# Mixture-of-experts blocks written to their tokens' places from inside the loop, with the second matrix read in place by TensorE

## The reference

```python
logits = t @ switch_w + switch_b
route_prob = softmax(logits); route_prob_max = max(route_prob); routes = argmax(route_prob)
for e in range(8):
    h = gelu(t @ w1[e] + b1[e])            # 128 -> 512
    y = h @ w2[e] + b2[e]                  # 512 -> 128
    out = where(routes == e, y, out)
out = out * route_prob_max                 # and then x = x + out
```

## Time and profile before

| what | value |
|---|---|
| time, median of 3 runs (lowest to highest) | 1508.23 us (1506.53 to 1508.61) |
| the profiled execution: its own time | 1510.94 us |
| the profiled execution: span from first to last instruction | 1509.1 us |
| TensorE busy | 1114.1 us (74%) |
| VectorE busy | 970.7 us (64%) |
| ScalarE busy | 696.1 us (46%) |
| GpSimd busy | 519.0 us (34%) |
| granted TensorE clock, mean | 0.871 of full speed |
| layer 0: scatter, loop, gather and norm | from 212.8, 254.5, 350.4 to 410.3 us |
| layer 1: scatter, loop, gather and output | from 1322.9, 1364.6, 1461.9 to 1509.1 us |

### The profile page before, as it was taken

The page is one execution under the profiler, slowest core; times in us unless marked ns, Lnnn a source line. Parts: engine busy times, 40 slices in busy tenths (PEclk is TensorE's granted clock), DMA queues, the critical chain, the costliest instruction groups (busy, mean ns, idle before and its releaser), DMA issues. The chain is left out here.

```text
span 1509.1 us, 31316 instructions
## 1 busy us (share of the span) xinstructions
PE 1114.1 (74%) x9281; PEld 992.8 (66%) x9281; DVE 970.7 (64%) x2930; ACT 696.1 (46%) x1448; POOL 519.0 (34%) x396
## 2 busy tenths in 40 slices
PE   3595321992264799999999999999999997607960
PEld 2494221881133698988889888898888985506850
DVE  6886930553472677787777777777787776503532
ACT  2144510551171466666666666666666663103430
POOL 1500125005200544444444444444444441071016
PEclk9998555996585999999999999999999998557985
DMA  8000031221068464746546465564655610211113
GB/s 220 0 0 1 1 143 47 61 57 49 26 232 220 114 154 119 163 121 140 145 125 161 113 150 134 129 162 111 158 131 129 158 33 2 112 61 53 56 52 99
DMA packets 85256, 156.21 MB, mean 104 GB/s; under 512 B 9056, under 2 KB 65824, under 8 KB 76512
## 3 DMA queue, kind: packets, MB, share of 16 engines
q1 hardware_dynamic: 81120, 147.33, 37.6%
q0 software_dynamic: 4096, 8.40, 1.9%
HBM read 127.51 MB, written 28.18 MB: 103 GB/s over the span
## 5 line engine op out<-in xcount | busy, mean ns | idle before, releaser
L1109 POOL TENSOR_SCALAR ds_scores<-ds_scores,ds_max 128x256 f32<-128x256 f32 x256 | 348.5, 1361 | 396.1 <-DVE ds_max L1301 396.0
L1293 DVE TENSOR_TENSOR ds_p2c<-ds_bank,ds_p2c 128x512 f32<-128x512 f32 x256 | 175.8, 687 | 95.5 <-PE ds_bank L1146 95.5
L1242 ACT ACTIVATE all_xt<-ds_bank 128x512 f32<-128x512 f32 x256 | 152.9, 597 | 152.0 <-PE ds_bank L1164 152.0
L1137 PE MATMUL ds_bank<-ds_qr,ds_tab 128*128 128x128 f32 x1536 | 189.1, 277 | 21.6 <-DVE ds_qr L1277 19.9
L1137 PE MATMUL ds_bank<-ds_kr,ds_tab 128*128 128x128 f32 x1536 | 198.6, 276 | 0.6 <-ACT ds_p2c L1226 0.6
L1137 PEld LDWEIGHTS ds_bank<-ds_qr,ds_tab 128*128 128x128 f32 x1536 | 180.9, 194 | 23.5 <-issue 23.4
L1301 DVE CUSTOM_DVE_ANT_0 ds_scores<-ds_bank,ds_p2c 128x256 f32<-128x256 f32 x512 | 195.3, 417 | 0.2 <-DVE ds_p2c L1293 0.2
L1226 ACT ACTIVATE ds_c2p_t<-ds_bank 128x512 f32<-128x512 f32 x256 | 152.7, 596 | 91.7 <-PE ds_bank L1137 90.5
L1137 PEld LDWEIGHTS ds_bank<-ds_kr,ds_tab 128*128 128x128 f32 x1536 | 185.0, 193 | 1.0 <-issue 0.8
L1226 ACT ACTIVATE ds_p2c<-ds_bank 128x512 f32<-128x512 f32 x256 | 149.2, 597 | 54.2 <-PE ds_bank L1137 54.1
L1146 PE MATMUL ds_bank<-all_constants,ds_c2p_t 128*128 128x128 f32 x1024 | 157.6, 276 | 0.0
(11 more groups left out here) (236 smaller groups left out, 1711.5 us busy)
## 6 DMA issues: line engine op xcount, KB each, us to landing
ds_qr<-scratch_qk SPq DMA_DIRECT2D x32, 1024.0 KB, 10.9
ds_kr<-scratch_qk SPq DMA_DIRECT2D x32, 1024.0 KB, 13.7
ds_tab<-scratch_tables SPq DMA_DIRECT2D x64, 248.0 KB, 9.8
ds_qs<-scratch_q_parts SPq DMA_DIRECT2D x32, 288.0 KB
ds_ks<-scratch_k_parts SPq DMA_DIRECT2D x32, 288.0 KB
slots_in<-all_zero SPq DMA_DIRECT2D x2, 2560.0 KB, 15.4
0f_weights<-expert_rows SPq DMA_DIRECT2D x1, 4112.0 KB, 13.2
1f_weights<-expert_rows SPq DMA_DIRECT2D x1, 4112.0 KB, 13.3
```

Source lines behind the costliest of these rows:

```text
L1109: pool.tensor_scalar(S[b % NS][:, 1, :], S[b % NS][:, 1, :], mx[:, 2 * b + 1:2 * b + 2], None, ALU.subtract).then_inc(s_sub1, 1)
L1137: last = pe.matmul(pb[n % 2][:, a * P:(a + 1) * P], TAB[half][:, kind, c:c + P], mov[:, :].rearrange("p (b g s) -> p g b s", b=HALF, s=16) ...
L1242: act.activation(PT[b], pt2[:, :].rearrange("p (k s) -> p k s", k=2), ACT.Exp).then_inc(s_exp, 1)
L1293: dve.tensor_tensor(z, pt1[b % 2][:, :].rearrange("p (a k) -> p a k", a=2), z, ALU.add).then_inc(s_z, 1)
```

## The change

The change does these things:

- A row in the slots gets 258 numbers in place of 128: the normalised token, the token itself (`X_AT`), the count of tokens left (`LEFT_AT`: 4096 minus the token's own number, so that the zeros of a padding slot mean "none"), and its probability (`PROB_AT`). `XN`, `X` and the two columns become one tile, `rows`. The zero fill grows to the same width.
- In the loop VectorE's `result` has three operations in place of one: y plus bias as before, the token's number from `LEFT_AT`, and y times probability plus the token itself. The last waits for the first.
- GpSimd scatters each block's `y` by these numbers to its tokens' places in the loop (`store`), 40 indirect transfers with a bounds check that leaves out padding. The target is the output in layer 1 and a DRAM tensor `tokens` in layer 0. SP's stores to `slots_out` go, and so do the 32 gathers, the tile `G` and the 32 additions behind the loop.
- In layer 0 SP loads `X` back from `tokens` in four transfers, one for each group of the norm.
- SP's load of `xb` for block k waits until y(k-4) is written, where it waited for the transpose of k-4, as the additions read `xb` too.
- `WB` holds the first matrix and the biases (644 columns). TensorE reads the second matrix in `WA` at a register of its own, which it loads from `bexp` in each `down`.
- The experts' matrices arrive in three transfers in place of two, and the zero fill is issued behind the linear attention's weights.

Core of the diff (the two loads of a layer's matrices, the constant `left` and renamed arguments left out):

```diff
-W1_AT, W2_AT, B1_AT, B2_AT = 0, F, F + FC * D, F + FC * D + FC
-EXPERT_COLS = B2_AT + D
+W1_AT, B1_AT, B2_AT, W2_AT = 0, F, F + FC, F + FC + D
+COPY_COLS, EXPERT_COLS = W2_AT, W2_AT + FC * D
+
+
+X_AT, LEFT_AT, PROB_AT = D, 2 * D, 2 * D + 1
+ROW = 2 * D + 2
...
         def _(pool):
+            def store(g, i):
+                pool.wait_ge(s_y, UNROLL * g + i + 1)
+                pool.indirect_dma_start(tokens, bass.IndirectOffsetOnAxis(ap=token[i][:, 0:1], axis=0), y[i][:, :], None,
+                                        bounds_check=TOKENS - 1, oob_is_err=False).then_inc(s_out[i], 16)
             pool.wait_ge(s_cleared, 16)
             for t in range(TILES):
                 pool.indirect_dma_start(slots_in, bass.IndirectOffsetOnAxis(ap=slot[:, t:t + 1], axis=0),
-                                        norm.XN[:, t, :], None).then_inc(s_scat, 16)
-            for i in range(UNROLL):
-                pool.wait_ge(s_out[i], 16 * GROUPS)
-            for t in range(TILES):
-                pool.indirect_dma_start(G[:, t, :], None, slots_out,
-                                        bass.IndirectOffsetOnAxis(ap=slot[:, t:t + 1], axis=0)).then_inc(s_gath[t // GQ], 16)
+                                        rows[:, t, :], None).then_inc(s_scat, 16)
+            for k in range(BLOCKS):
+                store(k // UNROLL, k % UNROLL)
 
         @block.sync
         def _(sp):
             sp.wait_ge(s_scat, 16 * TILES)
 
-            def rows(g, i):
-                wait_over(sp, s_xt, UNROLL * (g - 1) + i + 1)
+            def load(g, i):
+                wait_over(sp, s_y, UNROLL * (g - 1) + i + 1)
                 sp.dma_start(xb[i][:, :], slots_in[bass.ds((UNROLL * g + i) * P, P), :]).then_inc(s_x[i], 16)
-            def store(g, i):
-                sp.wait_ge(s_y, UNROLL * g + i + 1)
-                sp.dma_start(slots_out[bass.ds((UNROLL * g + i) * P, P), :], y[i][:, :]).then_inc(s_out[i], 16)
-
-
-            def step(g, i):
-                rows(g, i)
-                if not isinstance(g, int) or g > 0:
-                    store(g - 1, i)
-
-            over_blocks(sp, step)
+            over_blocks(sp, load)
             for i in range(UNROLL):
-                store(GROUPS - 1, i)
-            if finish is not None:
+                sp.wait_ge(s_out[i], 16 * GROUPS)
+            if again:
+                back = tokens.rearrange("(t p) d -> p t d", p=P)
                 for q in range(TILES // GQ):
-                    sp.wait_ge(s_fin, GQ * (q + 1))
-                    sp.dma_start(finish[:, q * GQ:(q + 1) * GQ, :], X[:, q * GQ:(q + 1) * GQ, :]).then_inc(s_stored, 16)
-                sp.wait_ge(s_stored, 16 * (TILES // GQ))
+                    sp.dma_start(rows[:, q * GQ:(q + 1) * GQ, X_AT:X_AT + D], back[:, q * GQ:(q + 1) * GQ, :]).then_inc(s_back[q], 16)
...
             def down(g, i):
                 k = UNROLL * g + i
                 wait_over(pe, s_y, k - 1)
+                e = pe.value_load(bexp[0:1, bass.ds(k, 1)], min_val=0, max_val=E - 1)
                 for c in range(FC):
                     pe.wait_ge(s_g, FC * k + c + 1)
-                    last = pe.matmul(py[i % 2][:, 0:D], h[i % 2][:, c, :], WB[i][:, W2_AT + c * D:W2_AT + (c + 1) * D], start=(c == 0), stop=(c == FC - 1))
+                    last = pe.matmul(py[i % 2][:, 0:D], h[i % 2][:, c, :], WA[:, bass.ds(e, 1), W2_AT + c * D:W2_AT + (c + 1) * D].rearrange("p a n -> p (a n)"), start=(c == 0), stop=(c == FC - 1))
                 last.then_inc(s_yp, 1)
...
@@ -414,18 +409,23 @@
             def expert(g, i):
                 e = dve.value_load(bexp[0:1, bass.ds(UNROLL * g + i, 1)], min_val=0, max_val=E - 1)
                 wait_over(dve, s_y, UNROLL * (g - 1) + i + 1)
-                dve.tensor_copy(WB[i][:, :], WA[:, bass.ds(e, 1), :].rearrange("p a n -> p (a n)")).then_inc(s_wb, 1)
-
-            def rows(g, i):
+                dve.tensor_copy(WB[i][:, :], WA[:, bass.ds(e, 1), 0:COPY_COLS].rearrange("p a n -> p (a n)")).then_inc(s_wb, 1)
+
...
             def result(g, i):
-                dve.wait_ge(s_yp, UNROLL * g + i + 1)
+                k = UNROLL * g + i
+                dve.wait_ge(s_yp, k + 1)
                 wait_over(dve, s_out[i], 16 * g)
-                dve.tensor_tensor(y[i][:, :], py[i % 2][:, 0:D], WB[i][:, B2_AT:], ALU.add).then_inc(s_y, 1)
+                dve.tensor_tensor(y[i][:, :], py[i % 2][:, 0:D], WB[i][:, B2_AT:COPY_COLS], ALU.add).then_inc(s_yb, 1)
+                dve.tensor_scalar(token[i][:, :], xb[i][:, LEFT_AT:LEFT_AT + 1], -1.0, float(TOKENS), ALU.mult, ALU.add)
+                dve.wait_ge(s_yb, k + 1)
+                dve.scalar_tensor_tensor(y[i][:, :], y[i][:, :], xb[i][:, PROB_AT:PROB_AT + 1], xb[i][:, X_AT:X_AT + D],
+                                         ALU.mult, ALU.add).then_inc(s_y, 1)
...
-            for t in range(TILES):
-                if t % GQ == 0:
-                    dve.wait_ge(s_gath[t // GQ], 16 * GQ)
-                dve.scalar_tensor_tensor(X[:, t, :], G[:, t, :], prob[:, t:t + 1], X[:, t, :], ALU.mult, ALU.add).then_inc(s_fin, 1)
-                if finish is None and t % GQ == GQ - 1:
-                    dve.wait_ge(s_fin, t + 1)
-                    norm.vector(dve, t // GQ)
-            if finish is None:
+            if again:
+                for q in range(TILES // GQ):
+                    dve.wait_ge(s_back[q], 16)
+                    norm.vector(dve, q)
                 norm.vector(dve, norm.GROUPS)
...
@@ -527,6 +523,7 @@
             for j in range(2):
                 sp.dma_start(gain[:, j, :], w[f"g{j + 1}"].partition_broadcast(P)).then_inc(s_gb, 16)
                 sp.dma_start(bias[:, j, :], w[f"b{j + 1}"].partition_broadcast(P)).then_inc(s_gb, 16)
+            clear_slots(sp)
...
     x = dram["L0_attn_a_x"].rearrange("b (u p) d -> p (b u) d", p=P)
-    y = out.rearrange("b (u p) d -> p (b u) d", p=P)
+    y = out.rearrange("b s d -> (b s) d")
-        X = m.sb("x", [P, TILES, D])
+        rows = m.sb("rows", [P, TILES, ROW])
+        XN, X = rows[:, :, 0:D], rows[:, :, X_AT:X_AT + D]
...
-                sp.wait_ge(s_zero, 1)
-                for slots, s_cleared in zip(slots_in, s_clear):
-                    sp.dma_start(slots.rearrange("(p b) d -> p b d", p=P), zero[:, :].unsqueeze(1).to_broadcast([P, BLOCKS, D])).then_inc(s_cleared, 16)
...
+        def clear_slots(sp):
+            sp.wait_ge(s_zero, 1)
+            for slots, s_cleared in zip(slots_in, s_clear):
+                sp.dma_start(slots.rearrange("(p b) d -> p b d", p=P), zero[:, :].unsqueeze(1).to_broadcast([P, BLOCKS, ROW])).then_inc(s_cleared, 16)
```

More of the change, by code:

```diff
@@ L269, in _, with run_experts @@
             then(dve.tensor_scalar(bexp[:, :], bexpf[:, :], float(E - 1), None, ALU.min))
-def run_experts(nc, prefix, X, norm, con, WA, s_weights, prob, slot, bexp, slots_in, slots_out, s_cleared, finish):
+def run_experts(nc, prefix, rows, norm, con, WA, s_weights, slot, bexp, slots_in, tokens, s_cleared, again):
     with ExitStack() as stack:
@@ L278, in run_experts @@
         UNROLL = 4
-        WB = [m.sb(f"expert_{i}", [P, EXPERT_COLS]) for i in range(UNROLL)]
-        xb = [m.sb(f"xb_{i}", [P, D]) for i in range(UNROLL)]
+        WB = [m.sb(f"expert_{i}", [P, COPY_COLS]) for i in range(UNROLL)]
+        xb = [m.sb(f"xb_{i}", [P, ROW]) for i in range(UNROLL)]
         xbt = [m.sb(f"xbt_{i}", [P, P]) for i in range(2)]
@@ L283, in run_experts @@
         y = [m.sb(f"y_{i}", [P, D]) for i in range(UNROLL)]
-        G = m.sb("gathered", [P, TILES, D])
+        token = [m.sb(f"token_{i}", [P, 1], U32) for i in range(UNROLL)]
         bank = m.banks(8)
         px, ph, py = bank[0:2], bank[2:4], bank[4:6]
-        if finish is None:
+        if again:
             norm.begin(bank[6:8])
-        s_fin, s_stored = m.sem("finished"), m.sem("stored")
-        s_wb, s_xt, s_xtc, s_h, s_g, s_yp, s_y = (m.sem(n) for n in ("wb", "xt", "xtc", "h", "gelu", "yp", "y"))
+        s_wb, s_xt, s_xtc, s_h, s_g, s_yp, s_yb, s_y = (m.sem(n) for n in ("wb", "xt", "xtc", "h", "gelu", "yp", "yb", "y"))
         s_scat = m.sem("scattered", own=True)
         GQ = norm.GT
-        s_gath = [m.sem(f"gathered{q}", own=True) for q in range(TILES // GQ)]
+        s_back = [m.sem(f"back{q}", own=True) for q in range(TILES // GQ)]
         s_x = [m.sem(f"x{i}") for i in range(UNROLL)]
-        s_out = [m.sem(f"out{i}") for i in range(UNROLL)]
+        s_out = [m.sem(f"out{i}", own=True) for i in range(UNROLL)]
         GROUPS = BLOCKS // UNROLL
@@ L1429, in shape_constants @@
         "iota_b": np.broadcast_to(np.arange(BLOCKS), (P, BLOCKS)),
+        "left": TOKENS - row[:, None] - P * np.arange(TILES)[None, :],
     }
@@ L1463, in program @@
         logits = m.sb("logits", [P, TILES, E])
-        zero = m.sb("zero", [P, D])
+        zero = m.sb("zero", [P, ROW])
         s_zero = m.sem("zero")
-        slots_in = [nc.dram_tensor(f"slots_in{layer}", (SLOTS, D), FP32, kind="Internal").ap() for layer in range(2)]
```

(3 more changed lines are left out.)

47 lines of the change are left out of this document (23 added, 24 removed).

## The result

The changed kernel takes 1460.05 us (median of 4 runs, 1458.41 to 1461.5) against 1508.42 for the one before: ratio 0.967, 95% interval 0.965 to 0.970. It is 48 us faster; I had forecast 64.

A forecast was written before the change was run, and what follows sets the result against it. It took a circle of TensorE and VectorE to bound the loop. Start -1, layer 0's tail -35.4, layer 1's -42.3 and loop +14.4 sum to -64.3 us, giving 1444 us; range 1424 to 1484.

The forecast's parts named there:

- the bound of the kernel before: Expert loop: a circle of TensorE and VectorE, 9.10 us for four blocks; whatever is added counts once for two blocks.
- the tails: Behind each layer's last result: without the gathers, 35.4 us saved in layer 0 and 42.3 in layer 1.
- VectorE's terms: Loop, each hop of two blocks: +0.35 us for the longer result, -0.30 for the narrower copy.
- the rivals with GpSimd: Loop: GpSimd's store holds VectorE's copy (1486 us, chance 0.15), or GpSimd itself becomes the bound (1460 us, chance 0.1).
- GpSimd becomes the bound: Loop: stores wait for VectorE to leave the memory port, 2.66 us a block, +16, 1460 us; chance 0.1.
- the step on the cover of the rows' load: Loop: rows lie there 5.0 us after up(k-3), the transpose needs them at 5.7; cover 0.7, so no cost.
- both of my terms: Loop: the later rows covered by 0.7 us, at no cost, and TensorE's register load at +0.31 us a hop.
- the transposes wait for rows: Loop: a sign that the prediction is wrong, if TensorE's transposes wait for the later-loaded rows.
- the register load of TensorE: Loop, ahead of down: the load alone, +0.31 us a hop; bounds 0 and 0.88.
- the start: Linear attention's start: zero fill moved behind its weights saves 1 us; 0 to 2 possible.

The follow-up runs named there:

- w2_copied: Changed kernel with VectorE copying all 1156 columns again and TensorE reading the second matrix from the copy without a register load: 1445.3 us, ratio 0.957.
- direct_store: Changed kernel with SyncE storing results block after block in slot order in place of GpSimd's indirect stores, the results' own places left out: 1449.4 us, ratio 0.959.
- in_place_only: Kernel before with only the second matrix read in place through TensorE's register load and VectorE copying 644 columns; gathers and stores as before: 1512.4 us, ratio 1.002.
- split_rows: Changed kernel with each block's rows loaded in two transfers, the transpose's 128 columns early, the rest when the result is written: 1443.0 us, ratio 0.956.
- before_fill_moved: Kernel before with only the zero fill, at its old width, issued behind the linear attention's weights: 1506.6 us, ratio 0.9992.

## Why the prediction was right, and where it was wrong

**Right: the bound of the kernel before, and the tails.** Without the gathers the tails got 34.9 us shorter (forecast 35.4) and 40.8 (42.3). Of the 1.5 missing in layer 1, 0.97 is the last store's later start and 0.6 the drain.

**Right: VectorE's terms.** Multiply-add 0.33 behind the addition (0.35 forecast), the narrower copy 0.27 less on the way to xbt (0.30), nothing held by the stores. w2_copied shows them in the period: 2.44 against 2.26 + 0.175.

**Right: the rivals with GpSimd are out.** The copy starts 0.86 behind the multiply-add's start (1.2 to 1.3 at the loop's turn, as in the kernel before) and takes 0.50; the stores take 1.04. That the time, 1460, is the one that I had worked out for "GpSimd becomes the bound" is chance: direct_store keeps layer 1's period without GpSimd. Part of it was also easier on the stores than I had thought: a store starts 0.79 behind the multiply-add's end and not 0.2, so it meets only the last 0.2 us of the copy. It takes 1.04 there, 0.98 with no copy beside it, and 1.29 in w2_copied, where the copy of 1156 columns runs beside it for some 0.5 us. That is 0.3 us more and lies in GpSimd's idle time. It is not the 2.5 more (3.1 in place of 0.62) that the Trainium skill ("SBUF — State Buffer", "SBUF: two separate sides") has beside a copy, whose length it does not give.

**Wrong: the step on the cover of the rows' load.** I wrote that the rows lie there 5.0 after up(k-3) and are needed 5.7 after it, a cover of 0.7. The load took 2.05, not 1.8, and the rows were about as late as I had them; the transposes started 0.67 behind the landing (median, 0.05 at the least). But I measured the cover at the transpose's place on the array. What the rows hold up is TensorE's queue, and behind the transpose stands the register load that the same change puts there, 0.86 us in its whole sequence. Needed is 0.99, there was 0.7, and so rows and load together became the bound. Priced each by itself, both of my terms nearly hold: in_place_only has 0.04 a block, where the terms gave 0.005, and split_rows 2.42, where I had forecast 2.46 for the loop without this wait. Together they cost 0.22 a block, 17 us, and the loop missed its forecast by 15.5. My sign for it, "the transposes wait for rows", was the wrong one too: of layer 1's transposes behind the first only three were held by their rows, two near the start by 0.1 us and the last by 1.2.

**Mis-sized: the register load of TensorE.** I took the TENSOR_LOAD of 0.31 alone, and named 0.88, the sequence, as a bound. What shows of it in the gap is 0.12 a block with the queue ahead (in_place_only), 0.39 with the queue held (changed). The row for its cover, no idle time ahead of down, held for a kernel whose rows came 2.5 us early. The Trainium skill gives TensorE's queue 64 instructions ("Advanced Engine Details and Errata", "Engine Queue Depths"), more than the 34 of a block; no run here shows that number.

**Mis-sized: the start.** The attention's first chunk came 1.1 us earlier, for the 1 us forecast. But as VectorE is held for whole operations of GpSimd, it became 6.9, of which before_fill_moved shows 4.3 in its profile and the rest is open. And 1.8 us went to the stretch from scatter to first up, which I had left as it was: 0.2 to the scatters with their longer rows and 1.6 to what stands between them and the loop.

**Luck.** On the profiled executions the sum missed by 13.9 us. The loop alone missed by 15.5, the tails by 2.0, that stretch by 1.8 and the rest by 0.5; the start gave back 5.9 that no term held.

## What to carry to other kernels

Measure a transfer's cover at the queue, not at the array: it ends at the waiting instruction, and everything behind that in program order, a register load above all, needs cover of its own. Where one change delays an input and lengthens what stands behind its wait, price the two together. If a load feeds both an early and a late reader, as the rows here, split it, so that the early part doesn't wait for the late one's buffer.
